# A convolutional LSTM whose three column blocks shift by one column a row, with its loops unrolled and its engines in another order

## The chip, the cores and the metric

The kernel runs on one core of one Trainium2 chip. The metric is device time in microseconds (us). A core has a matrix engine (TensorE, PE in the rows), a vector engine (VectorE, DVE), an activation engine (ScalarE, ACT), a general engine (GpSimd, POOL) and SyncE (SP), which issues the DMAs. Each works through its own list of instructions, and they meet through semaphores.

## The reference, cut to what matters

`x` is (32 images, 128 channels, 32 rows, 32 columns), float32. The network adds a normalised masked convolution with an LSTM over the rows to `x`, and then a normalised 3x3 convolution of the result.

```python
xs = conv(_gn(x), w_i2s * mask) + b_i2s          # 1 x 3 taps
x_rows = xs as (32 rows, 32 images * 32 columns, 128)

def step(carry, x_row):
    h, c = carry
    hc = conv(h, w_s2s, 1 x 3 taps, padding 1) + b_s2s
    gates = (x_row + hc) @ w_ih.T + bias
    i, f, g, o = split(gates, 4)
    c = sigmoid(f) * c + sigmoid(i) * tanh(g)
    h = sigmoid(o) * tanh(c)
    return (h, c), h

x = x + (the h of all rows)
x = x + conv3x3(_gn(x), W masked) + sum(b)
```

What matters here is that the three-tap convolution of `h` runs along all 32 * 32 = 1024 columns of a row as one line: column n of row t needs the columns n-1, n and n+1 of row t-1.

## The kernel before, in words

The kernel has three stages: the normalised input convolution, the LSTM, and the 3x3 convolution. Channels lie on the 128 partitions. The change touches the LSTM only, with the code that leads into and out of it.

A row of 1024 columns is cut into `NB = 3` blocks of 352, 320 and 352 columns (`BLOCKS`, whole images). Row and block make an *item*, 96 in all, numbered `it = 3 * row + block`; odd and even items use different buffers. In an item:

- ACT copies the input part `xs` into a PSUM bank (`load_xs`, L918). PE adds the state convolution onto it: nine float16 matmuls, three taps times three products of high and low halves. The taps that need only this block and the one to its left are `open_conv` (L1093, L1097), six matmuls; those that reach one column into the block to the right are `close_conv` (L1108 to L1113), three.
- ACT scales the sum into `z_hi` (L911), DVE makes the rest `z_lo` (L619). PE multiplies both with the gate weights: four gates of three matmuls with 32-bit operands, the first two gates (forget, input) in L1134 to L1138, the last two (candidate, output) in L1149 to L1151.
- ACT applies the sigmoid or tanh to the four gates (L930). The input gate stays in PSUM (`ps`), the other three go to SBUF (`gate`). POOL multiplies the forget gate with the old cell (`fc`, `forget`, L772). DVE multiplies input gate and candidate (`ps<-ps,gate`, L634), adds `fc` to the new `cell` (L638); ACT takes its tanh (`tc`, L937).
- DVE makes the state `hrow` from output gate and `tc` (L643), its float16 halves `hh` (L646) and `hl` (L648) for the next row's convolution, and the transposed `hT` (L653). POOL adds `hT` to the kept input `xr` and puts it into the image (`place`, L780).

Nothing schedules this: the order on an engine is the order in which its block of code issues. In the loop over pairs of rows every engine walks through its work of one item before it takes the next; only `open_conv` and `z_hi`, `z_lo` of the next item come early. PE runs `close_conv` of item `it`, `open_conv` of `it + 1`, and the twelve gate matmuls of `it`. `open_conv` waits for the state of its own block a row ago, `close_conv` for that of the block to the right, two items back in the order. `z_hi` and `z_lo` are single buffers.

The last item is issued apart, with statistics of the new image (`bn_stats`) between its steps, for the normalisation that begins the third stage.

Of the kernel before, what the change touches and what calls it, by code (L numbers as in the profile page):

```python
# [63 lines left out]
Z_AHEAD = 1  # L64
# [12 lines left out]
def width(k):  # L77
    return W * (BLOCKS[k][1] - BLOCKS[k][0])
# [11 lines left out]
def build_network(nc, x, w_i2s, b_i2s, w_s2s, b_s2s, w_ih, b_ih, b_hh, w_conv, b_conv, consts, out):  # L90
# [4 lines left out]
    with ExitStack() as ctx:  # L95
# [37 lines left out]
        with ExitStack() as s01:  # L133
# [282 lines left out]
        def _(v):  # L416
# [198 lines left out]
            def zlow(it, s, k):  # L615
                n = width(k)

                v.wait_ge(z_hi_done, it + 1)
                v.scalar_tensor_tensor(out=z_lo[:, 0:n], in0=zbank(s)[:, 0:n], scalar=z_unscale[:],  # L619
                                       in1=z_hi[:, 0:n].bitcast(F32), op0=ALU.mult,  # L620
                                       op1=ALU.subtract).then_inc(z_lo_done, 1)

            def item(j, s, last, final_step):
                u, k = s // NB, s % NB
                it = 2 * NB * j + s
                n = width(k)
                b0, b1 = BLOCKS[k]
                cols = slice(W * b0, W * b1)
                pads = slice(1 + W * b0, 1 + W * b1)
                p = s % 2  # L630

                v.wait_ge(gate_done, GATE_BANKS + GATES * it + 3)
                ig = gbank(s, 1)[:, 0:n]
                v.tensor_tensor(ig, ig, gate[p][2][:, 0:n], ALU.mult).then_inc(ig_done, 1)  # L634
                v.wait_ge(ig_done, it + 1)

                v.wait_ge(fc_done, it + 1)
                v.tensor_tensor(cell[:, cols], ig, fc[p][:, 0:n], ALU.add).then_inc(c_done, 1)  # L638
                if not last:
                    zlow(it + 1, s + 1, (k + 1) % NB)  # L640

                v.wait_ge(tc_done, it + 1)
                v.tensor_tensor(hrow[u][:, cols], gate[p][3][:, 0:n], tc[p][:, 0:n], ALU.mult).then_inc(h_done, 1)  # L643
                v.wait_ge(h_done, H_AHEAD + it + 1)
                if not final_step:
                    v.tensor_scalar(hh[u][:, pads], hrow[u][:, cols], ACT_SCALE, None, ALU.mult).then_inc(hh_done, 1)  # L646
                    v.wait_ge(hh_done, NB + it + 1)
                    v.scalar_tensor_tensor(out=hl[u][:, pads], in0=hrow[u][:, cols], scalar=ACT_SCALE,  # L648
                                           in1=hh[u][:, pads], op0=ALU.mult, op1=ALU.subtract).then_inc(hl_done, 1)

                v.wait_ge(row_done, it + 1)

                v.transpose(hT[p][:, 0:n], hrow[u][:, cols]).then_inc(ht_done, 1)  # L653

            zlow(0, 0, 0)
            with v.Fori(0, H // 2 - 1) as j:
                for s in range(2 * NB):
                    item(j, s, False, False)
            for s in range(2 * NB - 1):
                item(H // 2 - 1, s, False, s >= NB)  # L660
                if s >= 2:

                    v.wait_ge(row_done, ROW_AHEAD + NB * H // 2)
                    v.bn_stats(bn[:, s - 2, 0, :], image(s - 2)[:, 0:HW // 2]).then_inc(bn_done, 1)


# [18 lines left out]
            def lower_stats(b):  # L685
                v.bn_stats(bn[:, b, 1, :], image(b)[:, HW // 2:HW]).then_inc(bn_done, 1)
# [42 lines left out]
        def _(pool):  # L729
# [7 lines left out]
            pool.sem_inc(z_lo_done, Z_AHEAD)  # L737
# [46 lines left out]
            forget(0, 0)
            with pool.Fori(0, H // 4 - 1) as i:
                for slot in range(2):
                    for s in range(2 * NB):
                        forget(2 * i + slot + (s + 1) // (2 * NB), (s + 1) % (2 * NB))
                        place(2 * i + slot, s, slot, i + 1)
            for slot in range(2):  # L790
                j = H // 2 - 2 + slot
                for s in range(2 * NB):
                    if (slot, s) != (1, 2 * NB - 1):
                        forget(j + (s + 1) // (2 * NB), (s + 1) % (2 * NB))
                    place(j, s, slot, H // 4)
# [33 lines left out]
        def _(act):  # L829
# [76 lines left out]
            def high_z(it, s):  # L906

                n = width(s % NB)
                act.wait_ge(z_ready, it + 1)
                act.wait_ge(xs_loaded, it + 1)  # L910
                act.activation(z_hi[:, 0:n], zbank(s)[:, 0:n], ACT.Identity, scale=z_unscale[:]).then_inc(z_hi_done, 1)  # L911

            def load_xs(it, s, t):

                n = width(s % NB)
                b0, b1 = BLOCKS[s % NB]
                act.wait_ge(z_lo_done, Z_AHEAD + it - 1)
                act.activation(zbank(s)[:, 0:n].rearrange("p (b w) -> p b w", w=W), img32[:, b0:b1, t, :],  # L918
                               ACT.Copy).then_inc(xs_loaded, 1)
# [334 lines left out]
```

## Time and profile before

| | us |
|---|---|
| median of 3 runs | 685.17 (684.93 to 690.69) |
| the profiled execution | 688.73 |
| its span, first to last instruction | 686.9 |
| first stage, up to the first gate matmul at 122.45 | 122.45 |
| items 0 to 2 | 13.01 |
| items 3 to 93 | 323.54 |
| last two items, and the way into the third stage | 19.60 |
| third stage | 208.30 |

The span is what the rows below divide up; the execution's own time has 1.8 us more around it. A time in a row is counted from the start of the span.

### The profile page before, as it was taken

The numbers are of one execution on the slowest core, as the hardware profiler recorded it, in microseconds if no ns is written. First come the engines' busy times: TensorE is split into PE (matmuls) and PEld (weight loads), VectorE is DVE, ScalarE is ACT, GpSimd is POOL, SyncE is SP. The second block draws the span as 40 slices with busy tenths as digits, with TensorE's granted clock in tenths as the row PEclk, the third lists the DMA queues.
The fourth block names the chain that finished last, engine by engine and source line by source line (L and its number), as shares of the span: only waits on it lengthen the run. The fifth ranks groups of instructions, "written<-read, shape, count | busy, mean of one in ns | idle before, by whom it ended". The sixth has DMA issues, their size and how long they took to land.

```text
span 686.9 us, 15501 instructions
## 1 busy us (share of the span) xinstructions
PE 624.6 (91%) x4968; PEld 374.4 (54%) x4968; DVE 537.5 (78%) x1204; ACT 472.7 (69%) x838; POOL 411.5 (60%) x385
## 2 busy tenths in 40 slices
PE   1899899899999999999999999992799999899995
PEld 1344344677777777777777777761233333343332
DVE  4788964699999999999999999998476677767441
ACT  2688688788998889898888998885343344433320
POOL 2388767355555555555555555557677776767770
PEclk9999999999999999999999999996699999999999
DMA  9989920021444314443144440303789999898996
GB/s 218 250 228 262 210 26 2 11 40 22 61 61 61 45 16 61 61 62 50 18 54 61 61 56 18 49 1 65 194 254 280 267 281 273 242 287 260 272 268 170
DMA packets 96396, 88.95 MB, mean 129 GB/s; under 512 B 78240, under 2 KB 79520, under 8 KB 96288
## 3 DMA queue, kind: packets, MB, share of 16 engines
q1 hardware_dynamic: 89536, 70.00, 45.9%
q10 hardware_dynamic: 6816, 18.38, 9.7%
q8 instruction: 27, 0.44, 0.3%
q14 instruction: 17, 0.14, 0.1%
HBM read 35.07 MB, written 16.78 MB: 75 GB/s over the span
## 4 chain that ended last, share of the span: by engine, by line
PE 57%; DVE 14%; ACT 8%; issue 7%; SPq 6%; DMA 4%; POOL 1%; ACTq 1%; DVEq 0%; POOLq 0%
PE ps L1186 14%; PE ps L1134 6%; PE ps L1093 5%; PE ps L1176 4%; PE ps L1138 4%; DMA shifted<-pad 4%; SPq L371 4%; PE ps L1135 3%; PE ps L1038 3%; PE ps L1039 3%; PE ps L1150 3%; PE ps L1151 3%; PE ps L1149 3%; SPq L377 3%; PE ps L1097 2%
## 5 line engine op out<-in xcount | busy, mean ns | idle before, releaser
L772 POOL TENSOR_TENSOR fc<-gate,cell 128x352 f32<-128x352 f32 (+1 forms) x96 | 104.7, 1091 | 157.3 <-ACT gate L930 155.2
L807 POOL COPY shifted<-pad 32x1073 f32<-32x1073 f32 x128 | 137.5, 1074 | 54.8 <-DVE pad L675 48.3
L930 ACT ACTIVATE gate<-ps,gate_bias 128x352 f32<-128x352 f32 (+1 forms) x288 | 146.3, 547 | 2.9 <-PE ps L1138 1.0
L1186 PE MATMUL ps<-shifted,wt_hi 128*32 128x512 f16 x1536 | 109.1, 391 | 9.4 <-DMA shifted<-pad 9.4
L682 DVE SCALAR_TENSOR_TENSOR img<-ps,y_unscale,img 128x512 f32<-128x512 f32 x64 | 47.8, 747 | 71.0 <-PE ps L1186 70.8
L959 ACT ACTIVATE pad<-img,nbias,rstd 128x1024 f16<-128x1024 f32 x32 | 39.8, 1244 | 80.0 <-PE ps L1186 71.2
L780 POOL TENSOR_TENSOR img<-hT,xr 128x352 f32 (+3 forms) x96 | 87.0, 906 | 2.6 <-DVE hT L653 2.6
L751 POOL TENSOR_TENSOR lo<-xn,hi 128x1024 f16<-128x1024 f32 x32 | 68.0, 2134 | 30.4 <-ACT hi L862 29.8
L438 DVE BATCH_NORM_STATS2 bn<-img 128x6 f32<-128x512 f32 x120 | 75.9, 681 | 5.4 <-DMA img<-in_x_dram 5.4
L1134 PE MATMUL ps<-z_hi,wg_hi 128*128 128x352 f32 (+1 forms) x192 | 70.4, 370 | 8.8 <-ACT z_hi L911 2.8
L1186 PEld LDWEIGHTS ps<-shifted,wt_hi 128*32 128x32 f16 x1536 | 35.2, 96 | 65.4 <-issue 22.9
L937 ACT ACTIVATE tc<-cell 128x352 f32<-128x352 f32 (+1 forms) x96 | 47.0, 490 | 26.5 <-DVE cell L638 26.5
L1150 PE MATMUL ps<-z_hi,wg_lo 128*128 128x352 f32 (+1 forms) x192 | 61.5, 320 | 0.0
L1151 PE MATMUL ps<-z_lo,wg_hi 128*128 128x352 f32 (+1 forms) x192 | 61.3, 319 | 0.0
L1149 PE MATMUL ps<-z_hi,wg_hi 128*128 128x352 f32 (+1 forms) x192 | 61.2, 319 | 0.0
L1135 PE MATMUL ps<-z_hi,wg_lo 128*128 128x352 f32 (+1 forms) x192 | 60.8, 320 | 0.0
L1134 PEld LDWEIGHTS ps<-z_hi,wg_hi 128*128 128x128 f32 x192 | 36.1, 188 | 42.0 <-issue 28.7
L634 DVE TENSOR_TENSOR ps<-ps,gate 128x352 f32<-128x352 f32 (+1 forms) x96 | 49.4, 515 | 10.2 <-ACT gate L930 8.5
L1176 PE MATMUL ps<-pad,wc_hi 128*128 128x512 f16 x128 | 51.5, 404 | 5.7 <-DVE pad L675 5.7
L643 DVE TENSOR_TENSOR hrow<-gate,tc 128x352 f32<-128x352 f32 (+1 forms) x96 | 49.4, 514 | 7.7 <-ACT tc L937 0.6
L1186 PE MATMUL ps<-shifted,wt_lo 128*32 128x512 f16 x768 | 54.3, 389 | 0.0
L619 DVE SCALAR_TENSOR_TENSOR z_lo<-ps,z_unscale,z_hi 128x352 fp32r<-128x352 f32 (+1 forms) x96 | 54.1, 563 | 0.2 <-ACT z_hi L911 0.2
(134 smaller groups left out, 1404.7 us busy)
## 6 DMA issues: line engine op xcount, KB each, us to landing
shifted<-pad SPq DMA_DIRECT2D x128, 134.1 KB, 4.1
shifted<-pad ACTq DMA_DIRECT2D x128, 134.1 KB, 4.2
xr<-in_x_dram SPq DMA_DIRECT2D x64, 256.0 KB, 5.7
img<-in_x_dram SPq DMA_DIRECT2D x126, 128.0 KB, 3.7
out_dram<-img SPq DMA_DIRECT2D x60, 256.0 KB, 4.5
shifted<-shifted SPq DMA_DIRECT2D x2, 553.5 KB, 6.0
out_dram<-img SPq DMA_DIRECT2D x16, 64.0 KB, 1.8
raw_c<-in_L_conv_W_dram SPq DMA_DIRECT2D x4, 144.0 KB, 3.2
```

Of the source, the lines that this page charges most:

```text
L438: v.bn_stats(bn[:, j, s, :], src[:, 512 * s:512 * s + 512]).then_inc(bn_done, 1)
L772: pool.tensor_tensor(fc[s % 2][:, 0:n], gate[s % 2][0][:, 0:n], cell[:, W * b0:W * b1], ALU.mult).then_inc(fc_done, 1)
L780: pool.tensor_tensor(img32[:, b0:b1, 2 * j + s // NB, :], hT[s % 2][:, 0:width(s % NB)].rearrange("p (b w) -> p b w", w=W), xr[:, slot, b0 ...
L807: pool.tensor_copy(shifted[b % SLOTS][32:64, q, ROWS_AT:ROWS_END].bitcast(F32), pad[b % SLOTS][32 * q:32 * q + 32, ROWS_AT:ROWS_END].bitca ...
L930: act.activation(gbank(s, m)[:, 0:n] if m == 1 else gate[p][m][:, 0:n], gbank(s, m)[:, 0:n], ACT.Tanh if gt == G_GATE else ACT.Sigmoid, bi ...
L1134: pe.matmul(gbank(s, m)[:, 0:n], wg_hi[:, GATE_ORDER[m], :], z_hi[:, 0:n], start=True, stop=False)
L1135: pe.matmul(gbank(s, m)[:, 0:n], wg_lo[:, GATE_ORDER[m], :], z_hi[:, 0:n], start=False, stop=False)
L1149: pe.matmul(gbank(s, m)[:, 0:n], wg_hi[:, GATE_ORDER[m], :], z_hi[:, 0:n], start=True, stop=False)
L1150: pe.matmul(gbank(s, m)[:, 0:n], wg_lo[:, GATE_ORDER[m], :], z_hi[:, 0:n], start=False, stop=False)
L1151: pe.matmul(gbank(s, m)[:, 0:n], wg_hi[:, GATE_ORDER[m], :], z_lo[:, 0:n], start=False, stop=True).then_inc(gate_ready, 1)
L1176: pe.matmul(y_bank(b, s).rearrange("p (h w) -> p h w", w=W), w[:], padded(pad[b % SLOTS], part, s, 0), start=(m == 0), stop=False, skip_gr ...
L1186: ins = pe.matmul(bank[32 * q:32 * q + 32], w[:, d, q, :], padded(shifted[b % SLOTS][:, q], part, s, d - 1), start=False, stop=(m == 2 and ...
```

## The change: shifted blocks, unrolled loops, other orders

A block's borders now lie one column further left in each row: row t has its borders at 351 - t and 703 - t (`EDGES`), so that the block widths run from 351, 352, 321 in row 0 to 320, 352, 352 in row 31. The column that a block reaches to its right a row ago is then its own, and the state convolution of an item needs the states of its own block and of those to the left. `open_conv` and `close_conv` become one `state_conv` of nine matmuls. Where a width is odd, the gate matmuls, `z_hi` and `z_lo` run over one column more (`even_width`, `offset`); `load_xs` copies the whole images that a block touches (`TOUCHED`: 11, 12 and 11 images), and `hT` and `place` keep to whole images (`PLACED`: 10, 11 and 11). All loops over the items are unrolled, `z_hi` and `z_lo` have two buffers each, and DVE, ACT and PE issue the steps of neighbouring items in another order. The state copies of the last row were left out before and still are.

```diff
-BLOCKS = [(0, 11), (11, 21), (21, 32)]
+PLACED = [(0, 10), (10, 21), (21, 32)]
+TOUCHED = [(0, 11), (10, 22), (21, 32)]
+EDGES = (351, 703)
+def columns(it):
+    t, k = it // NB, it % NB
+    return EDGES[k - 1] - t if k else 0, EDGES[k] - t if k < NB - 1 else B * W
-                z_hi = sb("z_hi", [P, 352], F32R, s1)
-                z_lo = sb("z_lo", [P, 352], F32R, s1)
+                z_hi = [sb(f"z_hi{i}", [P, WIDEST], F32R, s1) for i in range(2)]
+                z_lo = [sb(f"z_lo{i}", [P, WIDEST], F32R, s1) for i in range(2)]
...
+            for it in range(ITEMS + 1):
+                if it > 0:
+                    new_state(it - 1)
+                if it + 1 < ITEMS:
+                    zlow(it + 1)
+                if 0 < it <= ITEMS - NB:
+                    state_high(it - 1)
+                if it < ITEMS:
+                    input_gate(it)
+                if 0 < it <= ITEMS - NB:
+                    state_low(it - 1)
+                if it < ITEMS:
+                    new_cell(it)
+                if it > 0:
+                    turn_state(it - 1)
+                if ITEMS - CH <= it < ITEMS:
+                    if it == ITEMS - CH:
+                        v.wait_ge(row_done, ROW_AHEAD + NB * H // 2)
+                    upper_stats(it - (ITEMS - CH))
...
-            lower_stats(0)
-            v.bn_stats(bn[:, CH - 1, 0, :], image(CH - 1)[:, 0:HW // 2]).then_inc(bn_done, 1)
-            item(H // 2 - 1, 2 * NB - 1, True, True)
-            for b in range(1, CH):
+            for b in range(CH):
                 lower_stats(b)
...
+            forget(0)
+            for it in range(ITEMS + 1):
+                if it + 1 < ITEMS:
+                    forget(it + 1)
+                if it > 0:
+                    place(it - 1)
...
+            for it in range(ITEMS + 2):
+                if it > 1:
+                    cell_tanh(it - 2)
+                if it < ITEMS:
+                    high_z(it)
...
+                if 0 < it <= ITEMS:
+                    gate_of(it - 1, 2)
+                    gate_of(it - 1, 3)
+                if it + 2 < ITEMS:
+                    load_xs(it + 2)
+                if it < ITEMS:
+                    gate_of(it, 0)
+                    gate_of(it, 1)
...
+            def state_conv(it):
+                c0, c1 = columns(it)
+                u = (it // NB + 1) % 2
+                z = z_of(it)
+                pe.wait_ge(xs_loaded, it + 1)
+                pe.wait_ge(hh_done, it + 1)
                 for w in (ws_hi, ws_lo):
+                    for tap in range(3):
+                        pe.matmul(z, w[:, tap, :], hh[u][:, c0 + tap:c1 + tap], start=False, stop=False,
+                                  skip_group_check=True)
+                pe.wait_ge(hl_done, it + 1)
...
+            for it in range(ITEMS):
+                if NB <= it + 1 < ITEMS:
+                    state_conv(it + 1)
+                last_gates(it)
+                if it + 1 < ITEMS:
+                    first_gates(it + 1)
```

DVE in the middle of the LSTM, before: one item, from the product of input gate and candidate to the transposed state. L634 is that product, L638 the new cell, L619 is `z_lo` of the next item.

```order
L634 TENSOR_TENSOR ps<-ps,gate 128x320 [waits gate_done]
L638 TENSOR_TENSOR cell<-ps,fc 128x320 [waits fc_done,ig_done]
L619 SCALAR_TENSOR_TENSOR z_lo<-ps,z_unscale,z_hi 128x352 [waits z_hi_done]
L643 TENSOR_TENSOR hrow<-gate,tc 128x320 [waits tc_done]
L646 TENSOR_SCALAR hh<-hrow 128x320 [waits h_done]
L647 REGISTER_ALU
L648 SCALAR_TENSOR_TENSOR hl<-hrow,hh 128x320 [waits hh_done]
L653 STREAM_TRANSPOSE hT<-hrow 128x320 [waits row_done]
```

The same place after the change: L674 is `hrow`, L654 `z_lo`, L681 `hh`, L662 the product, L687 `hl`, L668 the cell and L695 `hT`.

```order
L674 TENSOR_TENSOR hrow<-gate,tc 128x337 [waits tc_done]
L654 SCALAR_TENSOR_TENSOR z_lo<-ps,z_unscale,z_hi 128x352 [waits z_hi_done]
L681 TENSOR_SCALAR hh<-hrow 128x337 [waits h_done]
L662 TENSOR_TENSOR ps<-ps,gate 128x334 [waits gate_done]
L687 SCALAR_TENSOR_TENSOR hl<-hrow,hh 128x337 [waits hh_done]
L668 TENSOR_TENSOR cell<-ps,fc 128x334 [waits fc_done,ig_done]
L695 STREAM_TRANSPOSE hT<-hrow 128x352 [waits row_done,h_done]
```

What stood one behind the other for one item (hrow, hh, hl; product, cell) now alternates with steps of another item, so that no instruction waits for the one just before it; `z_lo` moved from ahead of `hrow` to behind it.

ACT in the middle of the LSTM, before: the four gates of an item, `z_hi` of the next, the tanh of the cell, and the copy of the input part three items ahead.

```order
L930 ACTIVATE gate<-ps,gate_bias 128x320 [waits gate_ready]
L929 REGISTER_ALU
L930 ACTIVATE ps<-ps,gate_bias 128x320 [waits gate_ready]
L929 REGISTER_ALU
L930 ACTIVATE gate<-ps,gate_bias 128x320 [waits gate_ready]
L929 REGISTER_ALU
L930 ACTIVATE gate<-ps,gate_bias 128x320 [waits gate_ready]
L911 ACTIVATE z_hi<-ps,z_unscale 128x352 [waits xs_loaded,z_ready]
L936 REGISTER_ALU
L937 ACTIVATE tc<-cell 128x320 [waits c_done]
L918 ISA [waits z_lo_done]
L918 ACTIVATE ps<-img 128x320
```

The same place after the change: L981 is the tanh, L953 `z_hi`, L972 the gates, L961 the copy.

```order
L981 ACTIVATE tc<-cell 128x329 [waits c_done,h_done]
L953 ACTIVATE z_hi<-ps,z_unscale 128x344 [waits xs_loaded,z_ready]
L972 ACTIVATE gate<-ps,gate_bias 128x352 [waits gate_ready]
L972 ACTIVATE gate<-ps,gate_bias 128x352 [waits gate_ready,h_done]
L961 ACTIVATE ps<-img 128x384 [waits z_lo_done]
L972 ACTIVATE gate<-ps,gate_bias 128x343 [waits gate_ready]
L972 ACTIVATE ps<-ps,gate_bias 128x343 [waits gate_ready]
```

The tanh moved from behind `z_hi` to ahead of it and belongs to an item two back; the four gates of an item are parted, two ahead of the next turn and two behind its `z_hi`.

PE after the change, one turn: the state convolution of item `it + 1`, then the last two gates of item `it`, then the first two of `it + 1`.

```order
L1141 MATMUL ps<-hh,ws_hi 128x339 [waits hh_done,xs_loaded]
L1141 MATMUL ps<-hh,ws_hi 128x339 x2
L1141 MATMUL ps<-hh,ws_lo 128x339 x3
L1145 MATMUL ps<-hl,ws_hi 128x339 [waits hl_done]
L1145 MATMUL ps<-hl,ws_hi 128x339 x2
L1160 MATMUL ps<-z_hi,wg_hi 128x332 [waits gate_done]
L1160 MATMUL ps<-z_hi,wg_lo 128x332
L1165 MATMUL ps<-z_lo,wg_hi 128x332
L1160 MATMUL ps<-z_hi,wg_hi 128x332 [waits c_done,gate_done]
L1160 MATMUL ps<-z_hi,wg_lo 128x332
L1165 MATMUL ps<-z_lo,wg_hi 128x332
L1160 MATMUL ps<-z_hi,wg_hi 128x340 [waits gate_done,z_hi_done]
```

Six matmuls of the last gates now stand between a state convolution and the first matmul that needs its `z_hi`; before, the six of `open_conv` stood there.

## Rows read from the trace of the kernel before

**Rows 1.** Three stretches: length, busy PE, PEld, DVE, ACT, POOL, clock, DMA share, GB/s
```profile
122.45:135.46 13.01, 10.39 (x53) 8.27 (x52) 9.18 (x18) 9.21 (x20) 4.45 (x5) 0.87 0.09 10
135.46:459.00 323.54, 317.05 (x1911) 240.75 (x1912) 300.19 (x638) 290.87 (x637) 179.05 (x182) 1.00 0.33 46
...
478.60:686.90 208.30, 192.49 (x2524) 74.34 (x2524) 125.45 (x252) 74.19 (x68) 137.51 (x128) 0.96 0.88 254
```

**Rows 2.** Timeline of PE: start, duration, engine, line, operation, operands, count
```profile
302.12 0.46 PE L1097 MATMUL ps<-hl,ws_hi 128*128 128x352 f16 x2
...
302.62 0.42 PE L1134 MATMUL ps<-z_hi,wg_hi 128*128 128x352 f32 x1
...
302.88 0.32 PE L1135 MATMUL ps<-z_hi,wg_lo 128*128 128x352 f32 x1
...
303.04 0.32 PE L1134 MATMUL ps<-z_hi,wg_hi 128*128 128x352 f32 x1
...
304.81 0.31 PE L1110 MATMUL ps<-hh,ws_lo 128*128 128x352 f16 x1
...
304.96 0.31 PE L1113 MATMUL ps<-hl,ws_hi 128*128 128x352 f16 x1
```

**Rows 3.** Groups of DVE instructions by line, 200 to 450 us: busy, mean ns
```profile
L619 DVE SCALAR_TENSOR_TENSOR z_lo<-ps,z_unscale,z_hi 128x352 fp32r<-128x352 f32 (+1 forms) x71 | 40.0, 563 | 0.0
L653 DVE STREAM_TRANSPOSE hT<-hrow 128x352 f32<-128x352 f32 (+1 forms) x70 | 36.8, 526 | 0.0
L648 DVE SCALAR_TENSOR_TENSOR hl<-hrow,hh 128x352 f16<-128x352 f32 (+1 forms) x71 | 36.8, 518 | 2.4
L643 DVE TENSOR_TENSOR hrow<-gate,tc 128x352 f32<-128x352 f32 (+1 forms) x71 | 36.6, 515 | 5.4
L634 DVE TENSOR_TENSOR ps<-ps,gate 128x352 f32<-128x352 f32 (+1 forms) x70 | 36.0, 515 | 5.5 <-ACT gate L930 4.0
L638 DVE TENSOR_TENSOR cell<-ps,fc 128x352 f32<-128x352 f32 (+1 forms) x70 | 35.9, 513 | 2.4
L646 DVE TENSOR_SCALAR hh<-hrow 128x352 f16<-128x352 f32 (+1 forms) x71 | 24.3, 342 | 2.4
```

**Rows 4.** Timeline of DVE, and of ACT for its tanh, in one item
```profile
302.72 0.47 ACT L937 ACTIVATE tc<-cell 128x320 f32<-128x320 f32 x1 [0.23 <-DVE cell L638]
...
303.22 0.49 DVE L643 TENSOR_TENSOR hrow<-gate,tc 128x320 f32<-128x320 f32 x1
...
303.75 0.33 DVE L646 TENSOR_SCALAR hh<-hrow 128x320 f16<-128x320 f32 x1
...
304.11 0.50 DVE L648 SCALAR_TENSOR_TENSOR hl<-hrow,hh 128x320 f16<-128x320 f32 x1
...
304.52 0.50 DVE L653 STREAM_TRANSPOSE hT<-hrow 128x320 f32<-128x320 f32 x1
```

**Rows 5.** Timeline of ACT: its gates, back to back
```profile
304.17 0.52 ACT L930 ACTIVATE ps<-ps,gate_bias 128x352 f32<-128x352 f32 x1
...
304.61 1.00 ACT L930 ACTIVATE gate<-ps,gate_bias 128x352 f32<-128x352 f32 x2
```

**Rows 6.** ACT's group of z_hi, 200 to 450 us: busy, mean ns
```profile
L911 ACT ACTIVATE z_hi<-ps,z_unscale 128x352 fp32r<-128x352 f32 (+1 forms) x70 | 39.4, 563 | 0.0
```

**Rows 7.** Timeline of POOL and DVE: within an item, and in the last row
```profile
300.78 0.53 DVE L648 SCALAR_TENSOR_TENSOR hl<-hrow,hh 128x352 f16<-128x352 f32 x1
...
300.87 1.16 POOL L772 TENSOR_TENSOR fc<-gate,cell 128x320 f32<-128x320 f32 x1 [1.59 <-ACT gate L930]
...
461.32 0.87 POOL L772 TENSOR_TENSOR fc<-gate,cell 128x320 f32<-128x320 f32 x1 [2.04 <-ACT gate L930]
...
468.52 0.55 DVE L653 STREAM_TRANSPOSE hT<-hrow 128x352 f32<-128x352 f32 x1
468.99 1.83 DVE L686 BATCH_NORM_STATS2 bn<-img 128x6 f32<-128x512 f32 x3
469.15 0.93 POOL L780 TENSOR_TENSOR img<-hT,xr 128x352 f32<-128x352 f32 x1 [2.56 <-DVE hT L653]
```

More of the change, by code:

```diff
@@ L651, in item @@
-                v.wait_ge(row_done, it + 1)
[L653 to L664, printed above, removed]
+                v.tensor_tensor(hrow[it // NB % 2][:, c0:c1], gate[it % 2][3][:, 0:c1 - c0], tc[it % 2][:, 0:c1 - c0],
+                                ALU.mult).then_inc(h_done, 1)
@@ L784, in _, with place @@
[L784 to L795, printed above, removed]
+            def place(it):
+                b0, b1 = PLACED[it % NB]
+                t = it // NB
+                r = t // 2
+                pool.wait_ge(ht_done, it + 1)
+                pool.wait_ge(xr_in[r % 2], QUARTERS_IN * (r // 2 + 1))
+                pool.tensor_tensor(img32[:, b0:b1, t, :],
+                                   hT[it % 2][:, 0:W * (b1 - b0)].rearrange("p (b w) -> p b w", w=W),
+                                   xr[:, r % 2, b0:b1, t % 2, :], ALU.add).then_inc(row_done, 1)
@@ L904, in _, with high_z @@
             store_xs(B - 2)
-            def high_z(it, s):
-                n = width(s % NB)
+            def high_z(it):
                 act.wait_ge(z_ready, it + 1)
                 act.wait_ge(xs_loaded, it + 1)
[L911 to L919, printed above, removed]
@@ L921, in item @@
-            def item(j, s, last, loads):
-                it = 2 * NB * j + s
-                n = width(s % NB)
-                b0, b1 = BLOCKS[s % NB]
-                p = s % 2
-                act.wait_ge(h_done, it + 1)
-                for m, gt in enumerate(GATE_ORDER):
-                    act.wait_ge(gate_ready, GATES * it + m + 1)
-                    act.activation(gbank(s, m)[:, 0:n] if m == 1 else gate[p][m][:, 0:n], gbank(s, m)[:, 0:n],
-                                   ACT.Tanh if gt == G_GATE else ACT.Sigmoid,
-                                   bias=gate_bias[:, gt:gt + 1]).then_inc(gate_done, 1)
-                if not last:
-                    high_z(it + 1, s + 1)
+                act.activation(z_hi[it % 2][:, 0:even_width(it)], z_even(it), ACT.Identity,
+                               scale=z_unscale[:]).then_inc(z_hi_done, 1)
@@ L936, in item, with cell_tanh @@
+            def cell_tanh(it):
+                c0, c1 = columns(it)
+                act.wait_ge(h_done, it + 1)
                 act.wait_ge(c_done, NB + it + 1)
[L937 to L939 removed]
+                act.activation(tc[it % 2][:, 0:c1 - c0], cell[:, c0:c1], ACT.Tanh).then_inc(tc_done, 1)
             xs_stored(act, B - 4)
@@ new lines, in gate_bank_free, with gate_high, gate_low @@
+            def gate_bank_free(it, m):
+                pe.wait_ge(gate_done, GATES * it + m + 1)
+                if m == 3:
+                    pe.wait_ge(c_done, NB + it)
+            def gate_high(it, m):
+                n = even_width(it)
+                gate_bank_free(it, m)
+                for w in (wg_hi, wg_lo):
+                    pe.matmul(gbank(it, m)[:, 0:n], w[:, GATE_ORDER[m], :], z_hi[it % 2][:, 0:n], start=(w is wg_hi),
+                              stop=False)
+            def gate_low(it, m):
+                n = even_width(it)
+                pe.matmul(gbank(it, m)[:, 0:n], wg_hi[:, GATE_ORDER[m], :], z_lo[it % 2][:, 0:n],
+                          start=False, stop=True).then_inc(gate_ready, 1)
```

212 lines of the change are left out of this document (92 added, 120 removed).

## The prediction, made before the changed kernel ran

> **What bounds the kernel now.** I read the stretches first [rows 1]: the LSTM takes half the span, and the code before and behind it is the same in both kernels. Items 3 to 93 take 323.54 us with 1911 matmuls, 21 to an item, so 91 items at **3.555 us** each. PE counts as busy 317.05 us of it, but a matmul's duration overlaps the next one's, so that share says nothing of how dense PE is; the starts do. Next, the timeline of PE [rows 2]: 352 columns start 0.16 us apart with the gate weights (302.88 to 303.04) and 0.15 with the state weights (304.81 to 304.96). Twelve and nine of them are 3.27 us, and at the mean width of 341.3 columns (1024 / 3, in both kernels) **3.17**. PE therefore loses 0.38 us an item, and the same rows show where: of the two L1097 at 302.12 the next start is due at 302.42, the first gate matmul comes at 302.62, and the one behind it 0.26 later instead of 0.16. PE waits there for `z_hi`, which ACT makes behind the four gates of the item ahead.
>
> Behind that stands DVE. Its seven instructions of an item [rows 3] sum to 563 + 526 + 518 + 515 + 515 + 513 + 342 = 3.49 us. Two neighbours that don't depend on each other overlap by 0.09 (hl ends at 304.61, hT starts at 304.52), two that do stand 0.03 to 0.04 apart (hrow to hh, hh to hl) [rows 4]. In the old order three pairs depend on each other, and two more instructions wait for ACT, so the 3.49 come out as 3.55: DVE and ACT, handing one item to and fro, set the pace, and PE waits for them.
>
> **The change, part by part.**
>
> *Shifted blocks.* An item's convolution then needs states three items back at the nearest, not two. Nothing is saved in matmuls: 21 an item as before. Odd widths cost one column on a third of the items or so, under a nanosecond on the mean matmul. `load_xs` copies 12 images in place of 10 or 11 in the middle block, some 0.02 us of ACT an item, and ACT has room: it is busy 290.87 / 91 = 3.20 us an item now [rows 1], with seams that would close by 0.10 where its neighbours overlap as the gates do (0.44 from start to start, 0.52 long) [rows 5], so about 3.0 packed. `hh` writes float16 at odd columns already; whether it keeps its 342 ns over an odd column count no row shows, since all widths are even before. The bounds are 342 and the 518 ns of hl over the same columns [rows 3]: 0 to 0.18 us on a third of the items, 0 to 5 us in all. I take 0, since hh's own row is the nearest.
>
> *New orders.* All seven DVE seams can overlap now: 3.49 - 7 x 0.09 = 2.86. What remains is a ring through ACT, counted from the start of an item's cell. The cell takes 0.513, tc follows after 0.03 (taken as for tc to hrow, 303.19 to 303.22 [rows 4]) and takes 0.49 at the mean width, hrow follows at 1.06. ACT starts z_hi of the item two ahead 0.09 before tc ends, at 0.94; it takes 0.563 [rows 6], so z_lo starts at 1.54, later than hrow would let it. From there each DVE step takes its mean less 0.09: hh at 2.01, the product 2.26, hl 2.69, the next cell at **3.12**. PE's 3.17 is above it, so PE would set the pace if nothing else does.
>
> *PE's covers.* z_hi has the six matmuls of the last gates as cover, 0.93 us. From the last start of a convolution to PE's first gate matmul I count 0.31 for that matmul [rows 2], less the 0.15 after which the cover begins, 0.03 for the handover, 0.563 for z_hi and 0.13 for ACT to PE (an estimate: four handovers of 0.03): 0.88. So 0.05 us is left, and ACT must be free at that moment. If the cover is gone, PE pays the wait and 0.10 for the restart. The old state's last half hl ends at 3.21 after its cell; the convolution that needs it three items later gets to its hl taps at about 3.4. z_hi and z_lo in two buffers take away no wait that the rows show on PE; they let these orders stand.
>
> With three margins of 0.05 to 0.2 us in one ring, 3.17 won't be held; I take **3.25 us an item**, between 3.17 (all margins hold) and 3.40 (z_hi late by 0.1 and a restart in each item). 92 items from 3 to the end give 92 x (3.555 - 3.25) = 28.1 us, between 14 and 35.
>
> *Unrolling.* It saves the loop's branches and register steps, which are inside the 3.555. It makes more code to fetch: some 42 PE instructions in 3.25 us, 13 in a us. The third stage, unrolled already, runs 2 x 2524 in 208.3 us, 24 in a us, with the DMA engines 0.88 busy [rows 1], so I cost it at nothing.
>
> *Both ends.* Items 0 to 2 take 13.01 us with 53 matmuls, PE at 0.87 of its clock [rows 1]. They have no convolution, and in the new order gates of the next item don't wait for the state of this one: a gain between 0 and 3, I take 2. At the end four statistics instructions instead of three stand behind the last state, 1.83 / 3 = 0.6 each [rows 7]: 0.5 lost.
>
> The sum: 28.1 + 2 - 0.5 = 29.6 off the profiled execution's 688.73, or 659.1. That execution lies 3.56 above the median; taken off the median of 685.17 it is **655.6, say 656**, own range 648 to 669.
>
> **A rule that speaks against it.** POOL's fc, 320 wide, takes 0.87 in the last row, where no hl runs, and 1.16 where hl started 0.09 before it and runs 0.44 on [rows 7]: it stood still until hl was done, and hl itself takes its usual 0.53. So POOL waits for a DVE instruction with two inputs in SBUF. The old order never tests the reverse: hrow, hh and hl lie together in the stretch in which POOL waits for a gate. The new one spreads them, with POOL's two instructions (0.93 at 352 columns, 0.90 at the mean) between them.
>
> The Trainium skill, "SBUF — State Buffer", section "Who interferes with whom", states that the two engines share a port pair as an exclusive lock, and that whoever issues first holds it for the whole instruction while the other is fully blocked. By that rule the time is that of one of the next two rivals and not 656; the trace shows one side of it only.
>
> **The rivals.**
>
> *POOL holds up hh.* hT starts at 0.42 after the cell and ends at 0.95; `place` follows 0.08 later (469.07 to 469.15 [rows 7]), at 1.03, and hrow is due at 1.06. If hrow still goes first, POOL stands until hrow ends at 1.58 and then needs what it needs without the part hidden by the wait, 1.16 - 0.44 = 0.72, at the mean width 0.75: until 2.33. hh, due at 2.01, waits 0.32. The ring becomes 3.12 + 0.32 = 3.44: 92 x 0.115 + 1.5 = 12 us less, **673** (668 to 681). For it: the blocking that fc shows. Against it: that row fits a mere precedence of DVE as well.
>
> *POOL holds up hrow: slower.* If place goes first, 0.03 us being all that parts them, hrow waits until 1.03 + 0.90 = 1.93 instead of 1.06, z_lo starts at 2.36 instead of 1.54, and the ring grows by 0.82 to 3.94: 92 x 0.385 - 1.5 = 34 us more, **719** (700 to 740). It decides from the point at which place gets the port ahead of hrow. Against it: POOL seems to need some 0.15 before its data flow (0.87 against 0.72 above), in which hrow would pass it.
>
> *The margins don't hold.* The new ring is so tight that a late z_hi, a late state or a slow odd width gives back what the seams gain, or PE's wait only moves: 3.50 to 3.55 an item, **683** (678 to 688). For it: three waits due within 0.2 us of each other. Against it: DVE has 3.12 and ACT 3.0 of the 3.55.
>
> **How the numbers follow.** I give the forecast 0.48, POOL before hh 0.20, POOL before hrow 0.16, the margins 0.12, and 0.04 to anything else. The range reaches from 648 over the first, second and fourth, to **690**, and leaves out the slower rival. One per cent, 6.9 us, is about what a measurement of this kernel tells from no change. Faster by more, below 678.3: 0.48 + 0.15 of the second, 0.63. Within: 0.05 of the second and 0.11 of the fourth, 0.16. Slower: 0.16 and what is left, 0.21.
>
> **What would show it.** In the profile after: first matmuls of items 3.2 to 3.3 us apart; hrow to z_lo, hh to the product and hl to the cell overlapping by 0.09; the only idle time of DVE ahead of hrow and z_lo, ended by ACT; PE's wait ahead of the first gate matmul under 0.1. If POOL blocks DVE, hh or hrow start just as place or fc ends, with idle time ahead of them that no semaphore explains, and the items are 3.4 us or more. If the margins fail, PE's gap ahead of the gate matmuls or of the hl taps stays at 0.2 and more. The forecast is wrong if the pace is not set by PE and this ring, above all if POOL's port is.

## The result: slower, 702.36 us, and the profile after

The changed kernel takes **702.36 us** (median of 4 runs, 699.93 to 706.78), the kernel before 686.49 (684.93 to 690.69): a ratio of 1.0229, 95% interval 1.0157 to 1.0300. The forecast of 656 us and the range up to 690 are both missed, and the sign is wrong. The profiled execution took 699.93 us, its span 698.0. A time given for a kernel is the median of its runs; a ratio leaves out a run that is over 1.5% longer than the fastest of the same kernel, which below is one run of the place of one image and one of the four steps.

The same three stretches as in [rows 1], in the kernel after: items 0 to 2, items 3 to 93, third stage.

```profile
124.49:134.20 9.71, 8.97 (x45) 8.04 (x46) 5.45 (x12) 8.24 (x19) 3.35 (x4) 0.82 0.11 13
134.20:472.61 338.41, 313.91 (x1913) 243.78 (x1912) 321.73 (x639) 300.80 (x638) 167.84 (x183) 1.00 0.32 45
493.84:698.00 204.16, 190.66 (x2524) 73.83 (x2524) 125.16 (x252) 74.53 (x68) 137.48 (x128) 0.98 0.89 258
```

The 91 items take 338.41 us, 3.719 each, against 3.555 [rows 1]: **14.87 us lost**. Up to item 3 the kernel is 1.26 ahead (134.20 against 135.46), from item 94 to the third stage it loses 1.63 (21.23 against 19.60), and the third stage, the same code, is 4.14 shorter at a granted clock of 0.98 instead of 0.96. Together 11.1, the difference of the spans. So the question is the item.

Which instruction grew, the groups of DVE say, at 200 to 450 us of the kernel after (busy us, mean ns | idle us ahead):

```profile
L674 DVE TENSOR_TENSOR hrow<-gate,tc 128x352 f32<-128x352 f32 (+13 forms) x68 | 72.0, 1059 | 12.3 <-ACT tc L981 12.0
L654 DVE SCALAR_TENSOR_TENSOR z_lo<-ps,z_unscale,z_hi 128x352 fp32r<-128x352 f32 (+14 forms) x67 | 37.8, 564 | 0.1
L681 DVE TENSOR_SCALAR hh<-hrow 128x352 f16<-128x352 f32 (+13 forms) x67 | 24.8, 371 | 0.0
```

`hrow` went from 515 ns [rows 3] to 1059, `hh` from 342 to 371, and nothing else of DVE's grew: `z_lo` is at 564 against 563. No semaphore accounts for it, since the time is inside the instruction. What runs beside it, the timeline of the kernel after shows (two of POOL, DVE's instructions, and the gate matmuls of PE that wait for `z_lo`):

```profile
304.24 0.95 POOL L829 TENSOR_TENSOR img<-hT,xr 128x352 f32<-128x352 f32 x1
304.31 1.25 DVE L674 TENSOR_TENSOR hrow<-gate,tc 128x336 f32<-128x336 f32 x1 [0.16 <-ACT tc L981]
305.48 0.57 DVE L654 SCALAR_TENSOR_TENSOR z_lo<-ps,z_unscale,z_hi 128x352 fp32r<-128x352 f32 x1
305.98 0.32 DVE L681 TENSOR_SCALAR hh<-hrow 128x336 f16<-128x336 f32 x1
306.11 0.59 PE L1165 MATMUL ps<-z_lo,wg_hi 128*128 128x352 f32 x2 [0.34 <-DVE z_lo L654]
306.22 0.50 DVE L662 TENSOR_TENSOR ps<-ps,gate 128x335 f32<-128x335 f32 x1
306.63 0.50 DVE L687 SCALAR_TENSOR_TENSOR hl<-hrow,hh 128x336 f16<-128x336 f32 x1
307.05 0.50 DVE L668 TENSOR_TENSOR cell<-ps,fc 128x335 f32<-128x335 f32 x1
307.46 0.53 DVE L695 STREAM_TRANSPOSE hT<-hrow 128x352 f32<-128x352 f32 x1
...
308.16 0.51 DVE L674 TENSOR_TENSOR hrow<-gate,tc 128x335 f32<-128x335 f32 x1 [0.16 <-ACT tc L981]
308.18 1.29 POOL L829 TENSOR_TENSOR img<-hT,xr 128x352 f32<-128x352 f32 x1
308.63 0.57 DVE L654 SCALAR_TENSOR_TENSOR z_lo<-ps,z_unscale,z_hi 128x338 fp32r<-128x338 f32 x1
309.11 0.56 DVE L681 TENSOR_SCALAR hh<-hrow 128x335 f16<-128x335 f32 x1
...
311.50 0.87 POOL L829 TENSOR_TENSOR img<-hT,xr 128x320 f32<-128x320 f32 x1
311.57 1.19 DVE L674 TENSOR_TENSOR hrow<-gate,tc 128x352 f32<-128x352 f32 x1 [0.21 <-ACT tc L981]
```

Two kinds of item follow each other here. At 304.24 `place` (L829) starts 0.07 ahead of `hrow`: `place` takes its usual 0.95 and ends at 305.19, `hrow` ends at 305.56. At 308.16 `hrow` starts 0.02 ahead of `place`: `hrow` takes 0.51, and now `place` takes 1.29 and ends at 309.47; `hh`, which starts meanwhile, takes 0.56 and ends at 309.67. PE pays at 306.11, where it waits 0.34 for `z_lo`; before, its only gap was ahead of the first gate [rows 2]. From hrow to the next hrow it is 3.85 the first time and 3.41 the second. Over items 4 to 93 I count **71 items with a stretched hrow (median 1.23 us), 3.80 us each, and 19 with hrow at 0.51 and hh at 0.53, 3.40 each**; (71 x 3.80 + 19 x 3.40) / 90 = 3.72. These are the third and the second rival of the prediction, side by side in one run. The seams are as forecast: `z_lo` to `hh`, `hh` to the product, the product to `hl`, `hl` to the cell and the cell to `hT` overlap by 0.07 to 0.09.

### The profile page after: what moved, and what is told of

It is laid out like the page before. It is cut to its first block, busy times and chain, and to the rows that moved or that the text cites. A ratio compares the mean times of both kernels' runs of the same rounds, so it can differ in the third digit from the quotient of the medians.

```text
span 698.0 us, 14360 instructions
## 1 busy us (share of the span) xinstructions
PE 620.8 (89%) x4968; PEld 378.0 (54%) x4968; DVE 559.2 (80%) x1204; ACT 483.2 (69%) x838; POOL 400.5 (57%) x385
## 4 chain that ended last, share of the span: by engine, by line
DVE 36%; PE 23%; SPq 14%; ACT 11%; issue 9%; DMA 4%; POOL 1%; ACTq 1%; DVEq 0%; POOLq 0%
DVE hrow L674 13%; PE ps L1214 9%; SPq L406 8%; DVE z_lo L654 6%; ACT tc L981 6%; DVE cell L668 6%; SPq L412 5%; PE ps L1086 4%; PE ps L1087 4%; DMA shifted<-pad 3%; DVE hh L681 3%; PE ps L1204 2%; DVE hl L687 2%; ACT gate L972 2%; DVE bn L473 1%
## 5 line engine op out<-in xcount | busy, mean ns | idle before, releaser
L819 POOL TENSOR_TENSOR fc<-gate,cell 128x352 f32<-128x352 f32 (+16 forms) x96 | 83.8, 873 | 182.6 <-ACT gate L972 182.6
L972 ACT ACTIVATE gate<-ps,gate_bias 128x352 f32<-128x352 f32 (+32 forms) x288 | 153.2, 545 | 3.4 <-PE ps L1165 2.6
L1160 PE MATMUL ps<-z_hi,wg_hi 128*128 128x352 f32 (+13 forms) x384 | 135.9, 355 | 3.0 <-ACT z_hi L953 2.9
L1165 PE MATMUL ps<-z_lo,wg_hi 128*128 128x352 f32 (+13 forms) x384 | 115.2, 341 | 25.1 <-DVE z_lo L654 24.9
L1160 PE MATMUL ps<-z_hi,wg_lo 128*128 128x352 f32 (+13 forms) x384 | 122.4, 320 | 0.0
L674 DVE TENSOR_TENSOR hrow<-gate,tc 128x352 f32<-128x352 f32 (+16 forms) x96 | 99.0, 1031 | 18.2 <-ACT tc L981 16.9
L829 POOL TENSOR_TENSOR img<-hT,xr 128x352 f32<-128x352 f32 (+1 forms) x96 | 95.6, 996 | 3.2 <-DVE hT L695 2.2
L1165 PEld LDWEIGHTS ps<-z_lo,wg_hi 128*128 128x128 f32 x384 | 66.1, 189 | 45.8 <-DVE z_lo L654 45.7
L1160 PEld LDWEIGHTS ps<-z_hi,wg_lo 128*128 128x128 f32 x384 | 73.0, 190 | 0.0
L961 ACT ACTIVATE ps<-img 128x352 f32<-128x352 f32 (+1 forms) x96 | 45.6, 476 | 24.5 <-DVE z_lo L654 24.3
L654 DVE SCALAR_TENSOR_TENSOR z_lo<-ps,z_unscale,z_hi 128x352 fp32r<-128x352 f32 (+15 forms) x96 | 54.2, 564 | 3.3 <-ACT z_hi L953 3.0
L981 ACT ACTIVATE tc<-cell 128x352 f32<-128x352 f32 (+16 forms) x96 | 47.0, 490 | 14.1 <-DVE cell L668 7.9
L1141 PE MATMUL ps<-hh,ws_hi 128*128 128x352 f16 (+19 forms) x279 | 56.6, 311 | 0.1
```

The costliest lines, as they stand in the source:

```text
L654: v.scalar_tensor_tensor(out=z_lo[it % 2][:, 0:n], in0=z_even(it), scalar=z_unscale[:], in1=z_hi[it % 2][:, 0:n].bitcast(F32), op0=ALU.mul ...
L674: v.tensor_tensor(hrow[it // NB % 2][:, c0:c1], gate[it % 2][3][:, 0:c1 - c0], tc[it % 2][:, 0:c1 - c0], ALU.mult).then_inc(h_done, 1)
L819: pool.tensor_tensor(fc[it % 2][:, 0:c1 - c0], gate[it % 2][0][:, 0:c1 - c0], cell[:, c0:c1], ALU.mult).then_inc(fc_done, 1)
L829: pool.tensor_tensor(img32[:, b0:b1, t, :], hT[it % 2][:, 0:W * (b1 - b0)].rearrange("p (b w) -> p b w", w=W), xr[:, r % 2, b0:b1, t % 2, ...
L972: act.activation(gate_columns(it, m) if m == 1 else gate[it % 2][m][:, 0:n], gate_columns(it, m), ACT.Tanh if gt == G_GATE else ACT.Sigmoi ...
L981: act.activation(tc[it % 2][:, 0:c1 - c0], cell[:, c0:c1], ACT.Tanh).then_inc(tc_done, 1)
```

## The experiments

The theory: `hrow` reads two operands from SBUF, and while a POOL instruction that started ahead of it runs, it stands still; if hrow starts first, POOL stands until hrow is done, and `hh`, which starts while the delayed `place` still runs, pays later. The rivals: the new orders or the unrolled code are slow by themselves, or the cost is a matter of the operands and not of who comes first. Ten kernels ran; a ratio is to the kernel before on the same chip, and so is a time set against a run's.

**The output gate kept in PSUM.** hrow then reads one operand from SBUF; the order on each engine, the widths and the unrolled loops stay. With the bank, a wait for hrow moves from ACT, ahead of the fourth gate, to PE. At 200 to 450 us of the kernel after ACT shows no idle time at that wait, so its going takes nothing away.

```diff
-v.tensor_tensor(hrow[...], gate[it % 2][3][:, 0:c1 - c0], tc[...], ALU.mult)
+v.tensor_tensor(hrow[...], gate_columns(it, 3), tc[...], ALU.mult)
...
-act.activation(gate_columns(it, m) if m == 1 else gate[it % 2][m][:, 0:n], ...)
+act.activation(gate_columns(it, m) if m % 2 else gate[it % 2][m][:, 0:n], ...)
-if m == 3:
-    act.wait_ge(h_done, it + 1)
...
 pe.wait_ge(gate_done, GATES * it + m + 1)
+if m == 1:
+    pe.wait_ge(h_done, it + 1)
```

> The changed kernel with one edit: ACT leaves the output gate in its PSUM bank, so hrow reads one operand from PSUM and only tc from SBUF; PE waits for hrow before it writes that bank again. Nothing else moves, POOL's work is the same. Theory 'POOL's place holds the SBUF read port that hrow needs for its second input': hrow is back from 1.1 to 1.25 us to about 0.52 although place still runs over it, the items fall from 3.72 to 3.2 or 3.3 us, and the time to 650 to 665 us (92 items less 0.45 to 0.5). Rival 'hrow is slow for another reason of the new order, as ACT's writes of gates and tc beside it': hrow stays above 1 us, the time within 695 to 710.

Measured: **653.02 us** (650.42 to 657.54) against 688.71, ratio 0.9494 (0.9439 to 0.9549). The stretch of items 3 to 93, hrow's group, and the timeline of one turn:

```profile
133.76:425.31 291.55, 291.55 (x1913) 245.10 (x1912) 274.06 (x639) 287.63 (x638) 159.31 (x183) 1.00 0.36 52
```

```profile
L674 DVE TENSOR_TENSOR hrow<-ps,tc 128x352 f32<-128x352 f32 (+16 forms) x74 | 38.0, 513 | 12.6 <-ACT tc L978 12.1
```

```profile
302.33 0.53 DVE L695 STREAM_TRANSPOSE hT<-hrow 128x352 f32<-128x352 f32 x1
302.51 0.48 ACT L978 ACTIVATE tc<-cell 128x333 f32<-128x333 f32 x1
...
302.63 0.44 PE L1160 MATMUL ps<-z_hi,wg_hi 128*128 128x352 f32 x1
...
302.92 0.32 PE L1160 MATMUL ps<-z_hi,wg_lo 128*128 128x352 f32 x1
...
302.94 0.95 POOL L829 TENSOR_TENSOR img<-hT,xr 128x352 f32<-128x352 f32 x1
302.95 0.55 ACT L953 ACTIVATE z_hi<-ps,z_unscale 128x340 fp32r<-128x340 f32 x1
303.02 0.51 DVE L674 TENSOR_TENSOR hrow<-ps,tc 128x333 f32<-128x333 f32 x1 [0.16 <-ACT tc L978]
...
303.53 0.57 DVE L654 SCALAR_TENSOR_TENSOR z_lo<-ps,z_unscale,z_hi 128x340 fp32r<-128x340 f32 x1
...
304.02 0.33 DVE L681 TENSOR_SCALAR hh<-hrow 128x333 f16<-128x333 f32 x1
```

In the turn shown `place` starts 0.08 ahead of hrow and runs over all of it, and hrow takes 0.51. Over items 4 to 93 place starts ahead of hrow in 36 of 90, and hrow takes at most 0.53 in any of them: place ahead no longer holds it. `hh` still takes 0.33, but it starts only 0.07 (median) behind the end of place, so that this version keeps a small margin there and not a large one. An item takes 291.55 / 91 = **3.204 us**; PE counts as busy without a gap. The Trainium skill, in the section that the prediction cites, says that a DVE instruction with at most one input from SBUF and outside the modes that use two ports doesn't contend with POOL; this run agrees. The orders, the unrolling and the odd widths are fast; two operands of one instruction turned a gain of 5% into a loss of 2%. This version beats both kernels.

**A place of one image only.** It adds 32 columns in place of 320 or 352 and leaves the other images' sums out.

```diff
-pool.tensor_tensor(img32[:, b0:b1, t, :], hT[...][:, 0:W * (b1 - b0)], xr[..., b0:b1, ...], ALU.add)
+pool.tensor_tensor(img32[:, b0:b0 + 1, t, :], hT[...][:, 0:W], xr[..., b0:b0 + 1, ...], ALU.add)
```

> The changed kernel, with place shortened to the first image of its block (32 of 320 or 352 columns); the rest of the LSTM's output is left out of the image, so the result is another. POOL's instruction falls from 0.9 us to some 0.2. Port theory: hrow waits at most 0.2 us, items 3.2 to 3.35 us, 650 to 667 us. Rival 'hrow is slow for another reason': hrow stays above 1 us and the time at 695 to 710.

Measured: 655.28 us, ratio 0.9487 (0.9416 to 0.9558). hrow's operands are as in the change; only POOL's time went. Its group, and that of `place`, at 200 to 450 us:

```profile
L674 DVE TENSOR_TENSOR hrow<-gate,tc 128x352 f32<-128x352 f32 (+16 forms) x74 | 40.1, 542 | 12.6 <-ACT tc L981 11.9
L829 POOL TENSOR_TENSOR img<-hT,xr 128x32 f32<-128x32 f32 x75 | 35.8, 478 | 2.7 <-DVE hT L695 2.7
```

Changing either side, hrow's operands or POOL's time, makes the whole loss go. The 32 columns show 478 ns in the mean, since place waits where hrow is first.

**Place behind hrow.**

```diff
 pool.wait_ge(ht_done, it + 1)
+pool.wait_ge(h_done, H_AHEAD + min(it + 2, ITEMS))
```

> The changed kernel with one more wait: place waits until the hrow that is due beside it (of the next item) is done. Port theory with the lock held for the whole instruction: hrow is back at 0.52, but place now runs 0.9 us from there, into the time at which hh is due 0.45 to 0.5 later, so hh starts or ends 0.3 late; items 3.4 to 3.5 us, 670 to 682 us. If only instructions with two SBUF inputs are held up (hh has one, and runs two columns a cycle), hh stays at 0.34 and the items come to 3.2 to 3.3 us, 650 to 664 us. If POOL is not the cause: 695 to 710.

Measured: 697.15 us, ratio 1.0137 (1.0093 to 1.0180). One turn of it, with hl and the next fc (L819):

```profile
300.93 0.51 DVE L674 TENSOR_TENSOR hrow<-gate,tc 128x336 f32<-128x336 f32 x1 [0.16 <-ACT tc L982]
...
301.57 0.94 POOL L830 TENSOR_TENSOR img<-hT,xr 128x352 f32<-128x352 f32 x1 [0.91 <-DVE hT L695]
301.87 0.84 DVE L681 TENSOR_SCALAR hh<-hrow 128x336 f16<-128x336 f32 x1
...
303.04 0.49 DVE L687 SCALAR_TENSOR_TENSOR hl<-hrow,hh 128x336 f16<-128x336 f32 x1
...
303.25 1.09 POOL L819 TENSOR_TENSOR fc<-gate,cell 128x352 f32<-128x352 f32 x1 [0.74 <-ACT gate L973]
```

hrow is back at 0.51, and hh takes 0.84: the hold moved, as expected, but its price was 15 to 27 us too low. `place` starts 0.13 behind hrow's end and needs all of its 0.94, so it ends 1.07 behind hrow. Items take 3.645 us. `fc` starts 0.21 behind `hl` and takes 1.09, while `hl` takes its usual 0.49: the hold that [rows 7] showed is there in the new order too.

**Place in two halves.**

```diff
-pool.tensor_tensor(img32[:, b0:b1, t, :], ...).then_inc(row_done, 1)
+pool.tensor_tensor(img32[:, b0:bm, t, :], ...)
+pool.tensor_tensor(img32[:, bm:b1, t, :], ...).then_inc(row_done, 1)
```

> The changed kernel with place as two instructions of half the images each, the same bytes in all. Theory 'the port is held for one whole instruction': hrow waits only for the first half, 0.4 to 0.5 us, and takes some 0.8 us instead of 1.2; items 3.4 to 3.6 us, 673 to 692 us. Rival 'hrow shares the port with POOL's data, whatever the instructions are': hrow stays at 1.1 to 1.3 us and the time at 700 or, for POOL's second start-up, a little above.

Measured: 678.61 us, ratio 0.9849 (0.9815 to 0.9883). One turn:

```profile
302.75 0.53 POOL L830 TENSOR_TENSOR img<-hT,xr 128x160 f32<-128x160 f32 x1
302.83 0.82 DVE L674 TENSOR_TENSOR hrow<-gate,tc 128x337 f32<-128x337 f32 x1 [0.16 <-ACT tc L985]
303.24 0.87 POOL L833 TENSOR_TENSOR img<-hT,xr 128x192 f32<-128x192 f32 x1
```

hrow waits for the first half, to 303.28, and ends at 303.65; the second half, begun at 303.24, stands meanwhile. Over items 4 to 93 hrow is stretched in 71, as after the change, but to 0.81 us and not 1.23 (medians). The hold lasts for the one instruction, not for POOL's work as a whole.

**The gate in PSUM, in the kernel before.** The same edit as in the first experiment (but ACT keeps its wait for hrow), on the old order, where no POOL instruction runs beside hrow in any of the 96 items.

```diff
-v.tensor_tensor(hrow[u][:, cols], gate[p][3][:, 0:n], tc[p][:, 0:n], ALU.mult)
+v.tensor_tensor(hrow[u][:, cols], gbank(s, 3)[:, 0:n], tc[p][:, 0:n], ALU.mult)
...
```

> The kernel before, with the output gate kept in its PSUM bank, so that the product with tc reads one operand from SBUF. Theory (the gain of the first experiment comes from POOL's hold on hrow being gone, and from nothing else of that edit): in the order before, POOL waits for a gate while hrow runs, so there is nothing to take away, and hrow keeps its 515 ns: ratio 0.995 to 1.005, items of 3.55 us. Rival (an operand in PSUM makes hrow, ACT's gate or the hand-over of banks cheaper by itself, or DVE's place in the ring shorter): 0.1 us or more an item, 9 us, ratio 0.987 or below.

Measured: 688.34 us against 687.57, ratio 1.0009 (0.9980 to 1.0038), items of 3.557. The edit gives nothing where there is no collision; hrow's group at 200 to 450 us keeps the 515 of [rows 3]:

```profile
L643 DVE TENSOR_TENSOR hrow<-ps,tc 128x352 f32<-128x352 f32 (+1 forms) x71 | 36.5, 515 | 5.5
```

**The kernel before, its loops written out.**

```diff
-with v.Fori(0, H // 2 - 1) as j:
+for j in range(0, H // 2 - 1):
```

and so for ACT, POOL and PE.

> The kernel before, with its four loops over the rows written out and nothing else changed. Prediction's step (unrolling costs and gives nothing, the branches lie inside the 3.555 us of an item): ratio 0.993 to 1.003. Rival (code to fetch costs more than the branches, which would be a part of what the change lost): 0.05 to 0.2 us an item, 5 to 18 us, ratio 1.007 to 1.027. Other rival (the branches stall PE or DVE once in six items): 2 to 5 us less, ratio 0.993 or below.

Measured: 689.17 us, ratio 1.0023 (0.9994 to 1.0052), items of 3.582 in its profile: no difference that these runs can tell, as the prediction had it. A cost of up to 0.04 us an item stays possible.

**Place later by one, two, four and eight small steps.** Memsets of one column stand between place's wait and place, with n = 1, 2, 4 and 8; place's operands and work stay.

```diff
 pool.wait_ge(xr_in[r % 2], QUARTERS_IN * (r // 2 + 1))
+for k in range(n):
+    pool.memset(idle[:, k, it:it + 1], 0.0)
 pool.tensor_tensor(img32[:, b0:b1, t, :], ...
```

> After, with one POOL memset of one column (0.11 us by the rows of such memsets) put between place's wait for the transpose and place itself: place starts later by some 0.1 us, and its lead of 46 to 130 ns over hrow shrinks to about nothing. Theory (who starts first has the port for its whole instruction, and hrow behind place runs only when place has ended): the items fall in two kinds, some with hrow at 0.5 us and place stretched behind it, some with hrow at 1.1 to 1.2 as before; the time lies between 675 and 702 us. Rival (the hold is not a matter of who starts first but of the operands alone, so that a tenth of a microsecond moves nothing): hrow keeps 1.1 us or more in nearly all items, 702 to 712.

> After, with two such memsets ahead of place: place starts some 0.2 us later, so behind hrow in most items. Theory (who starts first holds the port): hrow is back at 0.52 us, place stands until hrow ends and then needs what is left of it, about 0.75, and hh, due 0.43 behind the end of hrow, starts while place runs and takes 0.5 to 0.8 instead of 0.33. That is the prediction's second rival, POOL before hh, with items of 3.35 to 3.5 us: 665 to 685 us. Rival (DVE goes first whenever both want the port, and only an instruction already running is left alone): hrow 0.52 and hh 0.33, items of 3.2 to 3.25, 653 to 660. Other rival (POOL goes first whenever both want it): hrow stays at 1.1 or more, 702 or above.

Measured: 699.36 us, ratio 1.0146 (1.0092 to 1.0200), and 697.17, ratio 1.0124 (1.0074 to 1.0173). The steps move place by less than expected (even four of them put it 0.21 behind the end of hT, where it stood at 0.09 after the change), and so the order flips in some items only: hrow is held in 71 of items 4 to 93 after the change, in 64 with one step, in 49 with two. In all three runs the held items take 3.80 to 3.84 and the free ones 3.39 to 3.40, so mainly the counts move the time. With two steps hrow is free where place starts up to 5 ns ahead of it or later (but for one item that fc holds up), and held where it starts 6 ns ahead or more. "Two steps" came out above its 665 to 685, because the steps were too short for the test, and not because of the theory.

> After, with four memsets of one column ahead of place (two of them took 0.14 us together in the last run, so about 0.2 here). After itself has two kinds of items: 69 of 90 where place starts 8 ns or more ahead of hrow (hrow 1.23 us, item 3.80) and 21 where hrow starts first (hrow 0.51, hh 0.53, item 3.45). Theory (who starts first holds the port): with hrow 0.05 to 0.15 ahead in nearly all items, the second kind is left, which is the prediction's second rival: items of 3.40 to 3.45, 0.28 to 0.32 less than the mean of 3.72, 92 items, 26 to 29 us: 669 to 680 us. Rival (the short items are short for another reason, as fc's own place, and hrow ahead doesn't bring them): 690 or above.

> After, with eight memsets ahead of place, about 0.35 us. Theory: place now starts inside hrow, so hrow's end alone frees it, and the extra delay costs nothing until place would start behind hrow's end: hh is held as with four, items of 3.40 to 3.45, 669 to 682 us. Rival (hh's wait follows place's start one for one even within hrow, since nothing of place is done under hrow): 0.15 us more an item than with four, 683 to 696.

Measured: **671.31 us**, ratio 0.9762 (0.9697 to 0.9827), and **672.53**, ratio 0.9775 (0.9720 to 0.9830). (The expectation counts by who starts first, 69 and 21 items; by hrow's duration it is 71 and 19.) One turn with four steps, then with eight:

```profile
301.02 0.51 DVE L675 TENSOR_TENSOR hrow<-gate,tc 128x337 f32<-128x337 f32 x1 [0.17 <-ACT tc L984]
301.08 1.26 POOL L832 TENSOR_TENSOR img<-hT,xr 128x352 f32<-128x352 f32 x1
...
301.97 0.58 DVE L682 TENSOR_SCALAR hh<-hrow 128x337 f16<-128x337 f32 x1
```

```profile
300.97 0.51 DVE L675 TENSOR_TENSOR hrow<-gate,tc 128x337 f32<-128x337 f32 x1 [0.16 <-ACT tc L984]
301.15 1.13 POOL L832 TENSOR_TENSOR img<-hT,xr 128x352 f32<-128x352 f32 x1
...
301.91 0.58 DVE L682 TENSOR_SCALAR hh<-hrow 128x337 f16<-128x337 f32 x1
```

hrow is free in 86 of 90 items of either kernel, an item takes 3.38 us, and the time is near the second rival's 673. POOL does more work here than after the change, and still the kernel takes 0.976 of the time before and not 1.023. Place starts 0.06 behind hrow in the one and 0.18 in the other, and ends 0.81 and 0.80 behind hrow's end: its start within hrow makes no difference here, as the theory says and the rival doesn't.

## Why the prediction was wrong

In the item of 3.25 us POOL's hold on DVE stands at nothing; it measured 0.72 us on hrow (0.51 to 1.23) in 71 of 90 items, and 0.2 on hh in the other 19. The step that put it at nothing is the weighing of "A rule that speaks against it", and within it one sentence of the third rival: "POOL seems to need some 0.15 before its data flow (0.87 against 0.72 above), in which hrow would pass it". Place and hrow were due 0.03 us apart (1.03 and 1.06 behind the cell), and this sentence let hrow win the tie. The runs show that it doesn't: whichever instruction starts first, by the trace, holds the other up until it is done, and a lead of some 10 ns is enough. The 0.15 itself is there (place ends 0.80 behind hrow where it takes 0.95 alone), but it is time that passes under the wait and lets nobody pass. The Trainium skill, "SBUF — State Buffer", section "Who interferes with whom", says that the one who issues first has the shared ports for the whole instruction, and that issue order decides who blocks; the trace agrees, with hrow at 1.23 us behind place and place at 1.29 behind hrow. The prediction had the rule, and gave 0.48 to the forecast, in which DVE passes POOL, on the ground that fc's row [rows 7] "fits a mere precedence of DVE as well". That row has one order of the two engines; it couldn't tell precedence from first come, first served, and where a row can't tell, the two should have been weighed by who starts first, here a tie. That it is one, the first experiment shows: with hrow free there, place starts first in 36 of 90 items. Why it does so in 69 of 90 after the change is not shown.

Its other steps, one by one:

- *The item of 3.25 us.* Right once the port is out of the way: 3.204 in the first experiment, 653.02 us against the forecast of 656; items 3 to 93 gave 32 us where 28 were forecast. PE as the bound holds: it shows no wait in these items there, and its 3.17 is nearly reached.
- *The seams.* Right: 0.07 to 0.09 where 0.09 was taken.
- *hh over odd widths.* Right at nothing: in the first experiment 0.33 at 335, 337 and 339 columns as at 334 to 340.
- *Unrolling at nothing.* Right within the 0.5% that the run can tell.
- *The second rival, 3.44 us and 673.* Near in both numbers where it is alone: 3.38 and 671.31. Its estimate that place needs 0.75 behind hrow's end measured 0.80; the wait of hh, 0.32 there, measured 0.23 (0.33 to 0.56).
- *The third rival, 3.94 us and 719.* The right mechanism, too large. hrow grows by 0.72 (0.51 to 1.23), not 0.87, since 0.14 of it passes under the wait: it ends 0.37 behind place and not 0.51. The ring grows by 0.05 less, since `z_lo` was due 0.05 after hrow would let it start: 3.12 + 0.67 = 3.79, where held items measured 3.80. And a fifth of the items fell to the second rival, by at most 33 ns, which is why 702 lies between the two.
- *Both ends, 1.5 gained.* Items 0 to 2 gained 3.30, but the first gate comes 2.04 later: in ACT's queue `z_hi` of item 0 now stands behind the waits for the last two images, ahead of them before. ACT's row in the kernel after shows the wait for DVE's copy of an image:

```profile
123.69 0.55 ACT L953 ACTIVATE z_hi<-ps,z_unscale 128x352 fp32r<-128x352 f32 x1 [2.10 <-DVE img L612]
```

  The end of the LSTM lost 1.63 with the port's hold and 0.18 without (first experiment, 19.78 against 19.60). In that experiment the way to item 3 is 1.70 shorter, so that both ends come to 1.52: the forecast's 1.5 was met there by luck, out of parts that were all off.
- *The sign to look for.* The prediction looked for hrow or hh starting just as place or fc ends, with idle time ahead. They start on time and last longer: the wait is inside the instruction's own duration.

The range shared the error: it ended at 690 because the one slower case with a mechanism had a chance of 0.16, where a tie of 0.03 us would have asked for about a half.

## What to carry to other kernels

When a new order lets two engines run at once that share a port, look at the operands of every pair that now overlaps, and at the difference of their due times; a tie is not a margin. Counting operands doesn't find every pair: hh reads a single one from SBUF and is held all the same, while `z_lo` (one from SBUF, one from PSUM) and `hT` (one) keep their 0.57 and 0.53 us when they start behind a POOL instruction. No run here isolates what sets hh apart. Where one operand of an instruction can come from PSUM at the same price (0.51 us for hrow either way), it takes the instruction out of the contest, and that is worth more here (0.949 of the time before) than shifting the other engine (0.976), which chooses who pays. An instruction that has grown is found in the group means first, since no wait shows it, and its cause in the timeline beside it.

## What the runs showed of the hardware

- The waiting instruction counts as busy while it stands. hrow behind place ends 0.37 to 0.38 us behind place's end (free it takes 0.51); hh behind place ends 0.19 to 0.21 behind it (free 0.33); place behind hrow ends 0.80 behind hrow's end (free 0.95). So about 0.14 of each has passed by the time the port comes free.
- The tie is decided within some 10 ns of the recorded starts: hrow is held in one item that it starts 4 ns ahead of place (one step), and free in two where place starts 5 ns ahead of it (two steps).
- The hold is of one instruction: between the two halves of a place, begun 0.04 ahead of the first one's end, hrow went first.
